# First attention layer: row minimum by a strided reduction, and the denominator of the own keys in an extra column of the context probabilities

## Time and profile before

| | |
|---|---|
| median of 3 runs | 2610.35 us (2606.86 to 2613.21) |
| span of the profiled execution | 2610.2 us; no time of its own is listed beside it |
| block 1, from the page's slices | about the first 700 us |
| TensorE, VectorE, ScalarE, GpSimd busy | 92%, 77%, 69%, 41% of the span |
| the page's costliest group in block 1 | L1947 GpSimd, 265.2 us busy |
| the next | L1743 ScalarE 175.4, L1453 VectorE 155.5, L991 TensorE 149.7 us |

### The profile page before, as it was taken

How to read it: one execution, slowest core, us unless ns; L and a number is a source line. 1 busy time by engine, 2 the same in 40 slices (tenths; PEclk the granted TensorE clock), 3 DMA queues, 4 the chain that set the end, 5 groups by cost and what they waited for, 6 DMA issues and landing times.

```text
span 2610.2 us, 43949 instructions
## 1 busy us (share of the span) xinstructions
PE 2395.8 (92%) x15754; PEld 1016.4 (39%) x15754; DVE 2016.2 (77%) x4111; ACT 1789.4 (69%) x3603; POOL 1080.0 (41%) x1342
## 2 busy tenths in 40 slices
PE   6999898998977899999999999999999999999877
PEld 3445454454522233333333333333333333333345
DVE  5777969878777788888888888887888888878434
ACT  4666657667435577777777777777777777777743
POOL 2544535545522344444344433444344444342322
PEclk9999999999958899999999999999999999999988
DMA  2000000000121222222212221212222222220000
GB/s 76 1 1 1 1 1 1 1 27 1 45 61 42 55 56 73 60 65 58 74 48 59 56 70 49 55 49 73 58 57 65 57 75 56 57 63 23 22 25 13
DMA packets 108562, 112.92 MB, mean 43 GB/s; under 512 B 15809, under 2 KB 96951, under 8 KB 107319
## 3 DMA queue, kind: packets, MB, share of 16 engines
q1 hardware_dynamic: 108345, 110.12, 15.5%
HBM read 14.80 MB, written 1.05 MB: 6 GB/s over the span
## 4 chain that ended last, share of the span: by engine, by line
PE 52%; DVE 26%; POOL 9%; issue 4%; ACT 4%; DMA 3%; SPq 2%; DVEq 0%; POOLq 0%; ACTq 0%
DVE A L1585 9%; PE psum L1110 7%; PE psum L1093 6%; PE psum L1081 5%; PE psum L1203 4%; PE psum L1016 4%; PE psum L1210 3%; DVE A L1607 3%; DMA A<-A 3%; PE psum L982 3%; PE psum L991 3%; DVE nm L1453 2%; PE psum L906 2%; POOL A L1978 2%; PE psum L1175 2%
## 5 line engine op out<-in xcount | busy, mean ns | idle before, releaser
L1585 DVE TENSOR_REDUCE A<-psum 128x1 f32<-128x512 f32 x1536 | 993.6, 683 | 206.9 <-PE psum L1093 202.2
L1802 ACT ACTIVATE A<-psum 128x512 f32<-128x512 f32 x1536 | 820.1, 599 | 270.9 <-PE psum L1081 138.3
L1093 PE MATMUL psum<-A 64*128 64x512 bf16 x1536 | 487.2, 395 | 49.2 <-DVE A L1585 36.1
L1081 PE MATMUL psum<-A 64*128 64x512 bf16 x1536 | 417.3, 387 | 19.3 <-ACT A L1802 12.7
L1110 PE MATMUL psum<-A 128*9 128x512 f32 (+1 forms) x3072 | 406.1, 606 | 1.0 <-ACT A L1811 0.2
L1947 POOL TENSOR_TENSOR A<-A,rden 128x512 f32<-128x512 f32 x256 | 265.2, 1058 | 253.8 <-DVE rden L1470 253.8
L1093 PEld LDWEIGHTS psum<-A 64*128 64x128 bf16 x1536 | 124.8, 96 | 375.5 <-DVE A L1585 331.3
L1832 ACT ACTIVATE A<-psum 77x512 f32<-77x512 f32 x384 | 204.2, 595 | 38.6 <-PE psum L1165 36.6
L1743 ACT ACTIVATE A<-psum,nm 128x512 f32<-128x512 f32 x256 | 175.4, 685 | 76.1 <-DVE nm L1456 75.3
L1978 POOL TENSOR_TENSOR A<-A 128x512 f32<-128x512 f32 (+1 forms) x78 | 96.8, 1241 | 306.0 <-DMA A<-A 306.0
L1081 PEld LDWEIGHTS psum<-A 64*128 64x128 bf16 x1536 | 105.9, 94 | 249.3 <-issue 101.8
(11 more groups left out here) (211 smaller groups left out, 3885.5 us busy)
## 6 DMA issues: line engine op xcount, KB each, us to landing
A<-A SPq DMA_DIRECT2D x456, 128.0 KB, 2.4
A<-A SPq DMA_DIRECT2D x336, 64.0 KB, 2.0
A<-zero SPq DMA_DIRECT2D x51, 128.0 KB, 2.3
wl<-in_wl SPq DMA_DIRECT2D x6, 1024.0 KB, 5.1
A<-A SPq DMA_DIRECT2D x36, 78.0 KB, 2.1
A<-in_nT SPq DMA_DIRECT2D x1, 1664.0 KB, 6.8
A<-in_w SPq DMA_DIRECT2D x2, 512.0 KB, 7.1
A<-in_w SPq DMA_DIRECT2D x1, 1024.0 KB, 6.1
```

The lines of the kernel that those rows point to most:

```text
L1081: handle.matmul(bank(b), k_st[bt][lo:lo + ROW, h // 2, k * P:(k + 1) * P], q_st[m % 3][lo:lo + ROW, h // 2, :], start=True, stop=True).the ...
L1093: handle.matmul(bank(b), q_st[m % 3][lo:lo + ROW, pair, q * P:(q + 1) * P], k_st[bt][lo:lo + ROW, pair, :], start=True, stop=True).then_in ...
L1585: handle.tensor_reduce(nm[:, pair // 4, q, j, pair % 4:pair % 4 + 1], bank(3 + j), AX.X, ALU.max, negate=True).then_inc(mx, 1)
L1802: handle.activation(pT[:, block % 2, i % GROUP, :], bank(ring_of["scores", m, i]), ACT.Exp, scale=HD1 ** -0.5).then_inc(ex, 1)
```

## The change

The maxima of the own scores and of the context get one common buffer, `mins`, of 4 + 8 slots of two heads: slots 0 to 3 for the steps in turn, slots 4 to 11 for the context maxima (two pairs x four query tiles). The second instruction of "maximum" becomes a tensor_reduce with min over a pair of slots, taken with the stride between them. c_p gets 78 words per (head, query tile) instead of 77; ScalarE's row sum of the own probabilities goes to the 78th word; the sum in "divide" runs over 78, and the addition of den goes. The wait for xp now stands before that sum. Transposes and GpSimd's multiply of the context leave the 78th word out.

```diff
-        c_p_raw = words(16 * C)
+        c_p_raw = words(16 * CP)
...
-        nm0, den, dsum = sb("nm0", [P, 4, 2]), sb("den", [P, 4, 2]), sb("dsum", [P, 2])
-        nmc = sb("nmc", [P, 2, 2, QT])
+        mins, nm0, dsum = sb("mins", [P, 4 + 2 * QT, 2]), sb("nm0", [P, 4, 2]), sb("dsum", [P, 2])
+        nmc = mins[:, 4:4 + 2 * QT, :].rearrange("p (n q) j -> p n j q", n=2)
...
-                        t = handle.transpose(psum[0:C, 4, q * P:(q + 1) * P], c_p[:, u % 2, j, q, :], ident[:, :])
+                        t = handle.transpose(psum[0:C, 4, q * P:(q + 1) * P], c_p[:, u % 2, j, q, 0:C], ident[:, :])
...
-                    handle.tensor_reduce(nm0[:, r, :], psum[:, s:s + 2, :], AX.X, ALU.max, negate=True).then_inc(own.next(), 1)
+                    handle.tensor_reduce(mins[:, r, :], psum[:, s:s + 2, :], AX.X, ALU.max, negate=True).then_inc(own.next(), 1)
                     dve.wait_ge(cs_m, NP0 * bt + u + 1)
                     after_own()
-                    handle.tensor_tensor(nm0[:, r, :], nm0[:, r, :], nmc[:, u % 2, :, q], ALU.min).then_inc(m0, 1)
+                    at = 4 + QT * (u % 2) + q
+                    handle.tensor_reduce(nm0[:, r, :], mins[:, r:at + 1:at - r, :].rearrange("p s j -> p j s"), AX.X, ALU.min).then_inc(m0, 1)
...
                     dve.wait_ge(dn, gi)
+                    dve.wait_ge(xp, 2 * gi + 2)
                     handle.tensor_reduce(dsum[:, :], c_p[:, n, :, q, :], AX.X, ALU.add).then_inc(own.next(), 1)
-                    dve.wait_ge(xp, 2 * gi + 2)
-                    after_own()
-                    handle.tensor_tensor(dsum[:, :], dsum[:, :], den[:, r, :], ALU.add).then_inc(own.next(), 1)
...
-                                      accum_out=den[:, r, j:j + 1]).then_inc(xp, 1)
+                                      accum_out=c_p[:, n, j, q, C:CP]).then_inc(xp, 1)
...
-                    handle.activation(c_p[:, n, j, q, :], c_sc[:, n, j, q, :], ACT.Exp, bias=nm0[:, r, j:j + 1]).then_inc(xc, 1)
+                    handle.activation(c_p[:, n, j, q, 0:C], c_sc[:, n, j, q, :], ACT.Exp, bias=nm0[:, r, j:j + 1]).then_inc(xc, 1)
...
-                    rows = c_p_raw.rearrange("p (n r t) -> p n r t", n=2, t=C)[:, i % 2, :, :]
+                    rows = c_p_raw.rearrange("p (n r t) -> p n r t", n=2, t=CP)[:, i % 2, :, 0:C]
```

## The result

The changed kernel takes 2573.05 us (median of 4, 2565.71 to 2577.67) against 2611.37 us beside it; the ratio is 0.9848, 95% interval 0.9822 to 0.9875. Run again with the later experiments it gave 2571.25 us and 0.9833 (0.9804 to 0.9862). The profiled execution spans 2571.9 us and took 2574.09 us.

What follows compares the result with a forecast made beforehand. VectorE was taken to be late in the first layer's attention, with TensorE's 40.5 us of idle time about the most to win. Of this 28.0 us, less 2 for GpSimd, give 2610.35 - 26 = 2584 us, range 2571 to 2598.

Steps and rivals of the forecast that it cites:

- The bound: First layer's attention: VectorE, though not 100% busy, is late and makes TensorE idle, 40.5 us in four stretches.
- The hold behind GpSimd: VectorE's two-input minimum waits until GpSimd's running instruction ends: 337 of its 497 ns.
- Rival (b): The reduction is held behind GpSimd too, or costs 305 ns: 2602 or 2590 us; chance 0.06.
- The price of the reduction: The minimum as a tensor_reduce on VectorE takes 150 ns, relieving VectorE of 44.4 us.
- The denominator: In "divide", summing a 78th column removes the addition and its wait: 27 us of VectorE over 128 steps.
- the cross-check: Attention's chain, 56 of 128 steps: 19.4 us for the minimum, 11.2 for the addition, 31 us at most.
- VectorE's busy time: VectorE loses 71 us of 521 in the attention; busy time before 700 us falls by 65 to 75.
- The share of TensorE's idle time: Four attention stretches: 76% of TensorE's idle time comes back, a third in the first; 28.0 us in sum.
- The 2 us taken off for GpSimd's multiply: TensorE's weight loads in the attention wait for GpSimd's multiply, late next; 2 us off the gain.
- Rival (a): In the attention TensorE takes over at once, waiting on GpSimd and ScalarE; 9 us gained, 2601 us; chance 0.10.
- rival (c): More comes than TensorE's visible idle time, as its "busy" hides stalls: 45 us, 2565 us; chance 0.06.
- Rival (d): Slower: changed rhythm opens gaps in the attention where TensorE's granted clock falls; 2629 us; chance 0.03.

Runs made afterwards that it cites:

- e3: Changed kernel plus a spare tensor_tensor behind each minimum, both inputs in SBUF, result unread: 2601.42 us, ratio 0.9966.
- e6: Kernel before with three instead of four transposes of the own probabilities per turn, so less TensorE work: 2604.80 us, ratio 0.9962.
- e4: Changed kernel plus a spare tensor_tensor ahead of each minimum, one input in PSUM and one in SBUF: 2573.44 us, ratio 0.9867.
- e8: Kernel before with GpSimd's multiply of the own probabilities over only 256 of 512 columns: 2582.21 us, ratio 0.9906.
- e1: Kernel before with only the minimum made a reduction, the addition of den kept: 2582.65 us, ratio 0.9897.
- e9: Changed kernel with GpSimd's multiply of the own probabilities over only 256 of 512 columns: 2565.79 us, ratio 0.9841.
- e2: Kernel before with only the denominators in the 78th column, the two-input minimum kept: 2598.62 us, ratio 0.9959.
- e5: Changed kernel with three instead of four transposes of the own probabilities per turn: 2555.68 us, ratio 0.9766.
- e7: Changed kernel with the quantiser's scale computed in three small VectorE instructions instead of four: 2570.27 us, ratio 0.9833.

## Why the prediction was right, and where it was short

- **The bound**: right. VectorE, not fully busy, set the pace: e3 puts the held time back on VectorE and loses most of the gain, though ScalarE is released ahead of it. The signs came as announced: the output projections at 192.55 and 353.85 us are 161.3 us apart, TensorE is busy for 97.4% between them, and ScalarE's wait for the minimum fell from 71.5 to 34.7 us (40 us to the end of the attention). e6 leans the same way, as TensorE has less to do there and still waits for VectorE, but its clock clouds it.
- **The hold behind GpSimd**: right, by four signs: all 67 long minima end with a GpSimd instruction, the new one takes a steady 157 ns, e3 against e4, and e8. Rival (b) is out.
- **The price of the reduction**: 150 ns taken, 157 measured. The slope through the two reductions gave 146 for four elements, 11 ns short.
- **The denominator**: 27 us of VectorE taken. The addition's 24.0 us and a gap went. The sum's mean rose by 5 ns, but e1 and e8, which still sum 154 elements, have 308 ns too, so two more columns cost no more than the 2 ns taken. By itself the denominator is worth 11 us of time, what the cross-check gave it.
- **VectorE's busy time**: 65 to 75 us less was announced; it fell by 2016.2 - 1953.7 = 62.5 us over the whole span and by 544.7 - 483.8 = 60.9 up to the last projection, below the announced range. Of the 71 us some 4 were the gap before the reciprocal, which isn't busy time. And neighbouring instructions overlap in the record: the durations added up fell by 65.6 us up to the last projection, but what lay over a neighbour counts once in the busy time.
- **The share of TensorE's idle time**: 28.0 us was the sum, 28.5 went. Within it the shares were off both ways: 8.1 instead of 9.3 us in the second stretch, 4.2 instead of 2.2 in the first.
- **The 2 us taken off for GpSimd's multiply**: not seen. The weight loads' wait for it in the second stretch fell from 11.6 to 8.1 us, and no part of the expected gain was lost to it. e9 shows that a cut of its length by four tenths would still give 4.6 us. Rival (a) is out.
- **What was mis-sized**: the prediction left out what TensorE's "busy" may hide, took its idle time for about the most that could come, and gave more than that only the chance of rival (c), 0.06, with 45 us in all. "Busy" shrank by 12.3 us: at most 6.8 from the granted clock, the rest probably stalls under modelled ends. 26 + 2 + 0.5 + 12.3 = 40.8 us is the measured gain of the stage. Behind it the profiled span gives 2.4 us back, inside the scatter there, and the median comes out 11 us under the forecast of 2584. It lies only 2 us inside the range and nearer to (c)'s 2565. The path was right, but three tenths of the stage's gain came by a term that the prediction put at nothing.
- **Rival (d)**: the clock was affected, the other way round: with the gaps closed it no longer fell. Its mean between 40 and 640 us goes with VectorE's lateness over all kernels: 0.97 in e6, 0.99 in the kernel before, e2 and e3, 1.00 in the changed kernel and in e1, e4, e5, e7, e8 and e9 (e1 and e4 with one spell of 3.4 us each). The kernel before has one profile only, and what the clock costs by itself no run isolates.
- **The two parts**: e1 and e2 sum to less than the whole, which I had expected the other way round. A hold that was removed in one place showed up at the next instruction that can be held; the clock may have had a share.

## What to carry to other kernels

If an instruction of VectorE has a longest run many times its shortest, it may be held inside the engine, and the profile counts that as busy; look for a GpSimd instruction that ends at the same moment. Where both of its inputs lie in SBUF, give it one input: a strided reduction over neighbours, or an operand left in PSUM, and do the same for the next such instruction on the way, as the hold moves on. The idle time of the engine that will bound next is no upper limit to the gain when its "busy" is modelled.

## What the runs showed of the hardware

- A tensor_reduce of 128x4 elements to 128x2 in SBUF takes 156 to 163 ns, beside a running GpSimd instruction or not (146 to 149 in e4, right behind the spare instruction); a tensor_tensor of 128x2 takes 148 to 165 ns where it isn't held, and up to 3361 ns held. The Trainium skill (SBUF — State Buffer, Who interferes with whom) names the two SBUF inputs as the condition; the runs agree (505 ns against 159 with one input in PSUM). Nine additions that ran unheld inside a 1.01-us GpSimd instruction of 128x4 elements show that its whole length does not hold.
- A page of the Trainium skill that advises against tensor_reduce on a hot path (VectorE: DVE Perf Modes, Rules for kernel authors) does not hold here: 157 ns replaced 497, of which 160 were the unheld time.
- The granted clock stayed at 2.4 GHz through the attention once TensorE's gaps had gone, where it had fallen twice before, for 13.6 us in all; with less work for TensorE in the kernel before (e6), it fell more, to a mean of 0.97 between 40 and 640 us (30.7 us at the 1.2 GHz level).
